# Moving three shared tiles of the first FFN behind its routed ones, with the attention's front steps re-placed around them

## The chip, the cores and the metric

One core of a Trainium2 chip runs the kernel. The metric is the device time of one execution in microseconds; here the median of three is given. The engines are TensorE (PE; its weight loads are PEld), VectorE (DVE), ScalarE (ACT), GpSimd (POOL) and SyncE (SP). SPq, ACTq and POOLq are instructions of an engine's queue that only issue DMAs. "L933" is line 933 of the kernel before.

## The reference

The block is x + 0.5 FFN(LN(x)), then x + attention(LN(x)), then x + 0.5 FFN(LN(x)), in float32, on 2 x 1024 tokens of width 128. The FFN has one shared expert and 7 routed ones of hidden width 352, of which each token uses two.

```python
def expert(h, g, u, d): return (silu(h @ g.T) * (h @ u.T)) @ d.T
def ffn(x):
    w = top2_normalised(softmax(x @ wr.T + rb))          # [tokens, 7], two non-zero
    return expert(x, sg, su, sd) + sum(w[:, e] * expert(x, rg[e], ru[e], rd[e]) for e in range(7))
def attention(x):
    v = x @ w_v + v_b
    q = (x @ w_q + q_b) @ w_k.T + k_b                      # keys are x itself
    scores = einsum(q, x) / sqrt(8)                        # 16 heads of 8, causal
    return softmax(scores) @ v @ c_proj_w + c_proj_b
x = x + 0.5 * ffn(layernorm(x)); x = x + attention(layernorm(x)); x = x + 0.5 * ffn(layernorm(x))
```

## The kernel before

**Tiles.** The 2048 tokens are 16 tiles of 128 and 4 chunks of 512. Chunks 0 and 1 are the first batch entry ("first half"), chunks 2 and 3 the second. Every engine has its own queue, written out in order by hand; between the queues there are only semaphores. Nothing is re-ordered at run time, so an instruction that waits holds all behind it on its engine.

**The FFN.** `ffn_pe`, `ffn_act` and `ffn_dve` walk the same 54 jobs (`JOBS`): 16 shared tiles ("s") and 38 routed ones ("r", `NJ`). In step q TensorE does the up projections of job q (`up_pe`, L899 to L901), the transposes of job q-1 (`act_tr_pe`, L919) and the down projection of job q-2 (`down_pe`, L933). `BEFORE[f]` says how many shared tiles run ahead of the routed ones: 16 (all) in the first FFN, 11 in the second. Other work is put in by step number: `FRONT_*` ahead of the step's job work, `BETWEEN_*` inside it, `BEHIND_*` after it.

**The routing.** The router's top two give each token two slots in lists sorted by expert. For each half GpSimd scatters the normalised rows to `z_rows` in memory: 32 indirect DMAs, 16 a half (`sort_pool`, L1174). Behind each but the first two of the 32 it runs a small memset as a pause (`pause_pool`, L1184). SP loads the sorted rows of each routed tile back (`rows_load_sp`, L1260). Tiles 0 to 9 need only the first half's sorts; tile 10 (`WHOLE`) and all after it need both. The tiles come in batches; `batch_at` gives the step in which a batch's rows are transposed (`rows_tr_pe`, L953). GpSimd scatters each routed result to `y_rows` (`scatter_pool`, L1197), the results come back (`results_load`, L1271) and are added with their weights: `mix_dve` for chunks 0 and 1, `weigh_both_act` and `add_both_pool` (L1138) for chunks 2 and 3.

**To the attention.** Each chunk's x is normalised (`n_stats` on VectorE, `n_z` on ScalarE), transposed (`n_tr`, L573), split in a high and a low part (`n_hi`, `n_lo`), and gives q (`q_pe`) and v (`v_pe`, L1508 to L1510, 12 matmuls a chunk). Queries and keys are stored to `q_stack` and `k_stack` and loaded in another layout. Chunks 0 and 1 do this inside the last FFN steps; chunks 2 and 3 need all routed results and do it inside the attention's prologue.

**The prologue** (`attn_pe`, `attn_dve`) is a ring of 54 entries `r` over four PSUM banks. TensorE makes scores (L1603), VectorE takes their maxima (L1756). Entries 0 to 37 are the first group's maxima; then come one of the next group, the two rows of maxima ("mrow", entries 39 and 40), and 13 more of the next group. `rows_load` brings the rows of maxima into the queries by DMA. `SECOND_PE` and `SECOND_DVE` say ahead of which entry a step of chunks 2 and 3 runs. From entry 45 TensorE also makes the main scores (`unit_pe`, L1646), and ScalarE takes the exponentials (L1815); from the fourth on, a score waits for the exponential three before it. Behind it the loop over 8 groups of heads runs.

```python
        if r == 2:
            e.wait_ge(K.A["qf"], 1)
        for step, c in SECOND_PE.get(r, ()):
            late_pe(K, 0, step, c)
        if r == UNITS_FROM:
            e.wait_ge(K.A["vev"], NCH)
            e.wait_ge(K.A["qf"], NCH)
```

ScalarE's queue at that place reads: end of the FFN, `v_act` of chunks 0 and 1, `results_load` of the second half, the scaling of its results, `n_z` and `n_hi` of chunks 2 and 3, `q_act(2)`, `keys_store(2)`, `q_act(3)`, `keys_store(3)`, `v_act` of 2 and 3, attention. SP's reads: keys and queries of chunks 0 and 1, their loads, `rows_load`, queries of chunks 2 and 3, and the clearing of the third key buffer.

Of the kernel before, what the change touches and what calls it, by code (L numbers as in the profile page):

```python
# [29 lines left out]
P = 128  # L30
# [52 lines left out]
BEFORE = (TT, 11)  # L83
# [16 lines left out]
ONE_AT_AGAIN = (46, NQ)  # L100
# [12 lines left out]
def batch_at(f, step):  # L113

    for b, (j, _) in enumerate(BATCHES):
        if step == BEFORE[f] + j - min(2 if f else b, 1 if j == WHOLE else 2):
            return b
    return None
# [136 lines left out]
MID_N_BANK, Q_BANK, V_BANK = (7, 6, 0, 1), (7, 6, 6, 4), (6, 4, 1, 0)  # L255
# [915 lines left out]
def sort_pool(K, f, g):  # L1171
# [4 lines left out]
    if g % TT > 0:  # L1176
        pause_pool(K, f == 1 and t < HALF)
# [335 lines left out]
def v_pe(K, c):  # L1513
    e = K.nc.tensor
    if c == 0:
        e.wait_ge(K.A["qf"], 2)
    elif c == 1:
        e.wait_ge(K.FF[0]["yev"], NQ)
    else:
        e.wait_ge(K.NS[1]["lo"], NCH)  # L1520
# [7 lines left out]
def q_pe(K, c):  # L1528
    e, cols = K.nc.tensor, slice(c * CHUNK, (c + 1) * CHUNK)
    e.wait_ge(K.NS[1]["lo"], c + 1)  # L1530
    if c >= 2:
        e.wait_ge(K.A["vev"], c - 1)
# [40 lines left out]
def stack_store(e, dram, part, c, src, s):  # L1573
    b, half = c // 2, c % 2
    dst = dram[b * HEADS:(b + 1) * HEADS, 8 + 8 * part:16 + 8 * part, half * CHUNK:(half + 1) * CHUNK]
    e.dma_start(dst, src.bitcast(F32)).then_inc(s, 16)  # L1576


def keys_store(K, e, c):
    cols = slice(c * CHUNK, (c + 1) * CHUNK)  # L1580
    e.wait_ge(K.NS[1]["lo"], c + 1)
    stack_store(e, K.k_dram, 0, c, K.zt_h[1][:, cols], K.k_st[c])
    stack_store(e, K.k_dram, 1, c, K.zt_l[1][:, cols], K.k_st[c])
    stack_store(e, K.k_dram, 2, c, K.zt_h[1][:, cols], K.k_st[c])


def queries_sp(K, c):
    e, u = K.nc.sync, c % 2
    e.wait_ge(K.A["ql"], c + 1)
    stack_store(e, K.q_dram, 0, c, K.q_h[:, u, :], K.q_st[c])  # L1590
    stack_store(e, K.q_dram, 1, c, K.q_h[:, u, :], K.q_st[c])
    stack_store(e, K.q_dram, 2, c, K.q_l[:, u, :], K.q_st[c])
# [122 lines left out]
SECOND_PE = {4: (("v", 0),), 6: (("v", 1),), 29: (("n_tr", 2),), 34: (("n_tr", 3), ("q", 2)), 40: (("q", 3),), 41: (("v", 2),),  # L1715
             43: (("v", 3),)}
SECOND_DVE = {22: (("n_stats", 2),), 25: (("n_stats", 3),), 31: (("n_lo", 2),), 37: (("n_lo", 3),)}
# [3 lines left out]
def attn_pe(K):  # L1721
    e = K.nc.tensor
    for r, (what, d, n) in enumerate(RING_PROLOGUE):
# [4 lines left out]
        elif r == 2:  # L1728
            e.wait_ge(K.A["qf"], 1)
# [629 lines left out]
```

## Time and profile before

| | |
|---|---|
| time, median of 3 (lowest to highest) | 573.25 us (572.37 to 575.6) |
| the profiled execution's own time | 573.25 us |
| its span | 571.4 us |
| TensorE busy | 524.7 us, 92% |
| VectorE, ScalarE, GpSimd busy | 68%, 56%, 48% |
| chain that ended last | PE 58%, issue 22%, DVE 6%, DMA 6%, SPq 5% |

The page cuts the span in 40 slices of 14.3 us; each digit is the busy share in tenths.

```profile
PE   6988889999697789999999999999999889899995
DVE  5696635467249759788888888879465776445744
PEclk9799989999958979999999999999999999999999
DMA  8922324134830582505050505020000131340414
```

The first FFN fills slices 0 to 10, the attention 10 to 29, the second FFN 29 to 39. TensorE's row falls to 6 in slice 10 and to 7 in slices 12 and 13; the clock row falls to 5 in slice 11. The costliest groups of the page, with their count, busy time, mean of one, and the idle time ahead of them:

```profile
L1756 DVE TENSOR_REDUCE mxp<-psum 128x1 f32<-128x512 f32 (+3 forms) x304 | 179.8, 655 | 47.4 <-PE psum L1603 34.6
L1646 PE MATMUL psum<-queries,keys 128*128 128x512 f32 (+3 forms) x384 | 124.0, 385 | 4.0 <-ACT probs L1815 3.8
L1603 PE MATMUL psum<-keys,queries 128*128 128x512 f32 (+1 forms) x304 | 119.4, 428 | 7.6 <-DMA queries<-q_stack 5.3
L933 PE MATMUL psum<-wall_f,at 128*128 (+1 forms) x648 | 91.0, 277 | 2.5 <-DVE x L1081 1.3
```

### The profile page before, as it was taken

Reading aid. Unit: us, or ns where it says so; the run is one execution under the profiler, and the core shown is the slowest. Engines: PE = TensorE matmul, PEld = TensorE weight load, DVE = VectorE, ACT = ScalarE, POOL = GpSimd, SP = SyncE. Lnnn points to the kernel's source line nnn. Section 1 sums busy time; section 2 is a strip of 40 time slices with the busy share of each in tenths; the row PEclk is TensorE's granted clock in tenths of the full one; section 3 lists DMA queues with packets and bytes.
Section 4 is the critical chain, followed back from the end, with each engine's and each line's share of the span. In section 5 each row is a group of like instructions: output and inputs, shape, how many; then the busy total and the mean of one; then the engine's idle time right before and its main releaser. Section 6 shows DMA issues by size and latency. Waiting matters only on the chain.

```text
span 571.4 us, 11375 instructions
## 1 busy us (share of the span) xinstructions
PE 524.7 (92%) x3574; PEld 408.8 (72%) x3574; DVE 386.8 (68%) x1013; ACT 320.0 (56%) x678; POOL 272.6 (48%) x417
## 2 busy tenths in 40 slices
PE   6988889999697789999999999999999889899995
PEld 2788879988563566666665656565745889899995
DVE  5696635467249759788888888879465776445744
ACT  4553434457205377676676767677777334344643
POOL 8299888766425510204040404020237888864540
PEclk9799989999958979999999999999999999999999
DMA  8922324134830582505050505020000131340414
GB/s 284 290 73 60 101 80 121 44 103 119 255 102 24 179 192 75 175 1 175 1 175 1 175 1 168 9 101 2 2 2 24 34 86 48 101 117 31 127 49 120
DMA packets 41384, 54.65 MB, mean 96 GB/s; under 512 B 6064, under 2 KB 32176, under 8 KB 40560
## 3 DMA queue, kind: packets, MB, share of 16 engines
q1 hardware_dynamic: 31664, 41.13, 25.2%
q0 software_dynamic: 4480, 9.25, 4.9%
q10 hardware_dynamic: 5184, 3.55, 2.2%
q8 instruction: 32, 0.52, 0.4%
q14 instruction: 24, 0.20, 0.1%
HBM read 34.03 MB, written 28.00 MB: 109 GB/s over the span
## 4 chain that ended last, share of the span: by engine, by line
PE 58%; issue 22%; DVE 6%; DMA 6%; SPq 5%; ACT 1%; ACTq 1%; POOL 1%; DVEq 0%; POOLq 0%
PE psum L1603 12%; PE psum L1646 11%; PE psum L1675 10%; PE psum L933 6%; PE psum L919 3%; PE psum L899 3%; PE psum L900 3%; PE psum L901 3%; PE psum L1606 3%; DVE mxp L1756 3%; DMA b_p<-in_attn_c_proj_b 2%; SPq L1260 1%; SPq L1576 1%; DMA queries<-q_stack 1%; SPq L1253 1%
## 5 line engine op out<-in xcount | busy, mean ns | idle before, releaser
L1756 DVE TENSOR_REDUCE mxp<-psum 128x1 f32<-128x512 f32 (+3 forms) x304 | 179.8, 655 | 47.4 <-PE psum L1603 34.6
L1815 ACT ACTIVATE probs<-psum 128x512 f32<-128x512 f32 (+1 forms) x304 | 155.3, 578 | 32.9 <-PE psum L1646 30.1
L1646 PE MATMUL psum<-queries,keys 128*128 128x512 f32 (+3 forms) x384 | 124.0, 385 | 4.0 <-ACT probs L1815 3.8
L1603 PE MATMUL psum<-keys,queries 128*128 128x512 f32 (+1 forms) x304 | 119.4, 428 | 7.6 <-DMA queries<-q_stack 5.3
L1862 POOL TENSOR_SCALAR_AFFINE_SELECT probs<-probs 128x512 f32<-128x512 f32 x64 | 40.0, 634 | 174.9 <-ACT probs L1815 174.9
L1000 ACT ACTIVATE silu<-psum 128x352 f32<-128x352 f32 x107 | 49.5, 463 | 95.9 <-PE psum L901 70.7
L1043 DVE TENSOR_TENSOR act<-silu,psum 128x352 f32<-128x352 f32 x107 | 55.6, 519 | 64.9 <-ACT silu L1000 41.3
L1197 POOL DMA_INDIRECT y_rows<-ys,to_row x76 | 74.3, 977 | 52.2 <-DVE ys L1079 26.6
L933 PE MATMUL psum<-wall_f,at 128*128 (+1 forms) x648 | 91.0, 277 | 2.5 <-DVE x L1081 1.3
L1646 PEld LDWEIGHTS psum<-queries,keys 128*128 128x128 f32 x384 | 68.0, 194 | 30.2 <-ACT probs L1815 16.3
L933 PEld LDWEIGHTS psum<-wall_f,at 128*128 128x128 f32 x648 | 80.9, 192 | 4.0 <-issue 1.8
L1603 PEld LDWEIGHTS psum<-keys,queries 128*128 128x128 f32 x304 | 60.1, 200 | 23.8 <-DVE mxp L1756 8.2
L1675 PE MATMUL psum<-probs,vg 128*32 128x512 f32 (+3 forms) x768 | 69.8, 491 | 0.4 <-POOL probs L1862 0.4
L919 PE MATMUL psum<-ident,act 128*128 128x128 f32 x324 | 54.2, 276 | 6.7 <-DVE act L1043 5.8
L1008 ACT COPY at<-psum 128x384 f32<-128x384 f32 x108 | 51.3, 475 | 11.4 <-PE psum L919 10.2
L899 PE MATMUL psum<-wall,zs_h 128*128 x152 | 55.9, 368 | 1.7 <-DVE zs_l L1067 1.7
L900 PE MATMUL psum<-wall,zs_h 128*128 x152 | 49.7, 327 | 0.0
L919 PEld LDWEIGHTS psum<-ident,act 128*128 128x128 f32 x324 | 40.7, 141 | 12.5 <-DVE act L1043 8.6
L901 PE MATMUL psum<-wall,zs_l 128*128 x152 | 49.5, 326 | 0.0
L1675 PEld LDWEIGHTS psum<-probs,vg 128*32 128x32 f32 x768 | 21.1, 109 | 35.4 <-issue 22.3
L1174 POOL DMA_INDIRECT z_rows<-zrow,slots x32 | 34.6, 1081 | 15.1 <-DVE slots L750 9.7
L1174 POOL DMA_INDIRECT z_rows<-zrow_late,slots x32 | 31.2, 975 | 5.8 <-issue 5.8
(240 smaller groups left out, 737.9 us busy)
## 6 DMA issues: line engine op xcount, KB each, us to landing
z_rows<-q_stack SPq DMA_DIRECT2D x12, 682.5 KB, 5.5
keys<-k_stack SPq DMA_DIRECT2D x32, 128.0 KB, 6.3
queries<-q_stack SPq DMA_DIRECT2D x8, 512.0 KB, 6.0
zg_early<-z_rows SPq DMA_DIRECT2D x44, 65.0 KB
yc<-y_rows SPq DMA_DIRECT2D x10, 256.0 KB, 4.4
zg_late<-z_rows SPq DMA_DIRECT2D x32, 65.0 KB
q_stack<-q_h SPq DMA_DIRECT2D x8, 256.0 KB, 4.7
keys<-q_stack SPq DMA_DIRECT2D x4, 512.0 KB, 8.1
```

The source lines that it names most:

```text
L899: e.matmul(dst, zh, weight(K.wall, base, hi, HID), start=True, stop=False)
L900: e.matmul(dst, zh, weight(K.wall, base, lo, HID), start=False, stop=False)
L901: ins = e.matmul(dst, zl, weight(K.wall, base, hi, HID), start=False, stop=True)
L919: ins = e.transpose(bank(K, at_bank(f, q))[:, k * P:(k + 1) * P], K.act[:, q % 2, k * P:(k + 1) * P], K.ident[:, :])
L933: ins = e.matmul(bank(K, Y_BANK)[:, 0:EMB], K.at[:, q % 2, k * P:(k + 1) * P], weight(K.wall_f, base, DN + k * EMB, EMB), start=(k == 0), ...
L1174: e.indirect_dma_start(K.z_dram[f], bass.IndirectOffsetOnAxis(ap=K.slots[:, g:g + 1], axis=0), K.zrow[f][:, t, :], None).then_inc(K.z_sc[t ...
L1197: e.indirect_dma_start(K.y_dram[f], bass.IndirectOffsetOnAxis(ap=K.to_row[:, j:j + 1], axis=0), K.ys[:, j % RING_Y, :], None).then_inc(K.y ...
L1603: ins = e.matmul(dst, K.queries[u][:, i * P:(i + 1) * P], K.keys[u][:, heads[0]:heads[-1] + 1, k0 * P:(k0 + nb) * P], start=True, stop=Tru ...
L1646: ins = e.matmul(slot(K, u, d, n)[:, m * (q1 - q0):(m + 1) * (q1 - q0)], K.keys[v][:, j, kt * P:(kt + 1) * P], K.queries[v][:, q0:q1], sta ...
L1675: ins = e.matmul(bank(K, O_BANK)[32 * j:32 * j + 32, q0 - half * CHUNK:q1 - half * CHUNK], K.vg[:, kt, j, :], probs_of(K, n)[:, j, :], sta ...
L1756: e.tensor_reduce(K.mxp[:, heads[0]:heads[-1] + 1, i, which], scores, AX.X, ALU.max).then_inc(K.A["taken"], 1)
L1815: e.activation(probs_of(K, product)[:, heads[0]:heads[-1] + 1, :], src, ACT.Exp, scale=SCALE).then_inc(K.A["ex"], 1)
```

## The change

Thirteen shared tiles of the first FFN run ahead of the routed ones and three behind them, instead of all 16 ahead. Steps tied to routed results (mix, statistics, `n_tr`, q of chunks 0 and 1) stand three steps earlier. The v products of chunks 0 and 1 move from ring entries 4 and 6 into steps 50 and 51. The steps of chunks 2 and 3 move to earlier ring entries (19 to 32 instead of 29 to 43 on TensorE, 13 to 26 instead of 22 to 37 on VectorE). The batch of tile 10 is transposed two steps ahead of its first job rather than one. The first FFN's sorts lose their pauses. The key stores of chunks 2 and 3 are issued by SP, ahead of the query stores, and `rows_load` comes behind them all. The four additions of the projection's bias run on GpSimd ahead of the attention loop instead of inside it. PSUM banks and waits are altered to match.

```diff
-BEFORE = (TT, 11)
+BEFORE = (13, 11)
...
-ONE_AT_AGAIN = (46, NQ)
+ONE_AT_AGAIN = (43, NQ)
...
-        if step == BEFORE[f] + j - min(2 if f else b, 1 if j == WHOLE else 2):
+        if step == BEFORE[f] + j - (min(b, 2) if f == 0 else 1 if j == WHOLE else 2):
...
-MID_N_BANK, Q_BANK, V_BANK = (7, 6, 0, 1), (7, 6, 6, 4), (6, 4, 1, 0)
+MID_N_BANK, Q_BANK, V_BANK = (7, 6, 0, 1), (7, 6, 6, 4), (7, 6, 1, 0)
...
-    if g % TT > 0:
+    if f == 1 and g % TT > 0:
...
 def v_pe(K, c):
     e = K.nc.tensor
     if c == 0:
+        e.wait_ge(K.A["qf"], 1)
+    elif c == 1:
         e.wait_ge(K.A["qf"], 2)
-    elif c == 1:
-        e.wait_ge(K.FF[0]["yev"], NQ)
...
-    if c >= 2:
-        e.wait_ge(K.A["vev"], c - 1)
+    if c == 2:
+        e.wait_ge(K.A["vev"], 2)
+    elif c == 3:
+        e.wait_ge(K.FF[0]["yev"], NQ)
...
-def keys_store(K, e, c):
-    cols = slice(c * CHUNK, (c + 1) * CHUNK)
+def keys_sp(K, c):
+    e, cols = K.nc.sync, slice(c * CHUNK, (c + 1) * CHUNK)
...
-SECOND_PE = {4: (("v", 0),), 6: (("v", 1),), 29: (("n_tr", 2),), 34: (("n_tr", 3), ("q", 2)), 40: (("q", 3),), 41: (("v", 2),),
-             43: (("v", 3),)}
-SECOND_DVE = {22: (("n_stats", 2),), 25: (("n_stats", 3),), 31: (("n_lo", 2),), 37: (("n_lo", 3),)}
+SECOND_PE = {19: (("n_tr", 2),), 24: (("n_tr", 3), ("q", 2)), 29: (("q", 3),), 30: (("v", 2),), 32: (("v", 3),)}
+SECOND_DVE = {13: (("n_stats", 2),), 16: (("n_stats", 3),), 20: (("n_lo", 2),), 26: (("n_lo", 3),)}
...
-            e.wait_ge(K.A["qf"], 1)
+            e.wait_ge(K.A["vev"], 1)
...
-    e.wait_ge(K.NS[1]["z"], NCH)
-            if 0 <= 3 * p + u - 1 < NCH:
-                proj_bias_pool(K, 3 * p + u - 1)
...
-        keys_store(K, e, c)
+        keys_sp(K, c)
...
     queries_load(K, 0, 0, 1)
-    rows_load(K, 0, 0, 0, RING_PROLOGUE.index(("mrow", 0, 0)))
+    for c in range(NCH // 2, NCH):
+        keys_sp(K, c)
     for c in range(NCH // 2, NCH):
         queries_sp(K, c)
+    rows_load(K, 0, 0, 0, RING_PROLOGUE.index(("mrow", 0, 0)))
     for c in range(NCH // 2, NCH):
         e.wait_ge(K.k_st[c], 16 * 3)
         e.wait_ge(K.q_st[c], 16 * 3)
...
-def proj_bias_pool(K, c):
-    xc = K.x[:, c * TPC:(c + 1) * TPC, :]
-    K.nc.gpsimd.tensor_tensor(xc, xc, K.b_p[:, :].unsqueeze(1).to_broadcast([P, TPC, EMB]), ALU.add)\
-     .then_inc(K.A["bp"], 1)
+def proj_bias_pool(K):
+    e = K.nc.gpsimd
+    e.wait_ge(K.NS[1]["z"], NCH)
+    for c in range(NCH):
+        xc = K.x[:, c * TPC:(c + 1) * TPC, :]
+        e.tensor_tensor(xc, xc, K.b_p[:, :].unsqueeze(1).to_broadcast([P, TPC, EMB]), ALU.add).then_inc(K.A["bp"], 1)
...
-FRONT_PE = {10: (("places", 1),), 47: (("n_tr", 0),), 48: (("q", 0),), 50: (("n_tr", 1),), 51: (("q", 1),)}
-BETWEEN_ACT = [{0: (("query", 0), ("hi0", 2)), 1: (("hi0", 3),), 48: (("q", 0),), 51: (("q", 1),)}, {}]
+FRONT_PE = {10: (("places", 1),), 44: (("n_tr", 0),), 45: (("q", 0),), 47: (("n_tr", 1),), 48: (("q", 1),),
+            50: (("v", 0),), 51: (("v", 1),)}
+BETWEEN_ACT = [{0: (("query", 0), ("hi0", 2)), 1: (("hi0", 3),), 45: (("q", 0),), 48: (("q", 1),)}, {}]
-               20: (("tanh", 0),), 42: (("weigh", 0),), 44: (("weigh", 1),), 45: (("n_z", 0),), 46: (("n_hi", 0),),
-               47: (("n_z", 1),), 49: (("n_hi", 1),)},
+               20: (("tanh", 0),), 39: (("weigh", 0),), 41: (("weigh", 1),), 42: (("n_z", 0),), 43: (("n_hi", 0),), 44: (("n_z", 1),),
+              46: (("n_hi", 1),), 50: (("v", 0),), 51: (("v", 1),)},
-BEHIND_DVE = [{0: (("query", 0),), **{2 * k + 3: (("weights_lo", m),) for k, m in enumerate(ROUTED_WEIGHTS)}, 19: (("small", 0),), 22: (("weights", 0),), 42: (("mix", 0),), 43: (("n_stats", 0),), 44: (("mix", 1),), 45: (("n_stats", 1),),
-               46: (("n_lo", 0),), 48: (("q_lo", 0),), 49: (("n_lo", 1),), 51: (("q_lo", 1),)},
+BEHIND_DVE = [{0: (("query", 0),), **{2 * k + 3: (("weights_lo", m),) for k, m in enumerate(ROUTED_WEIGHTS)}, 19: (("small", 0),), 22: (("weights", 0),), 39: (("mix", 0),), 40: (("n_stats", 0),), 41: (("mix", 1),), 42: (("n_stats", 1),), 43: (("n_lo", 0),),
+              45: (("q_lo", 0),), 46: (("n_lo", 1),), 48: (("q_lo", 1),)},
...
-            v_act(K, 0)
-            v_act(K, 1)
...
-            keys_store(K, e, 2)
-            keys_store(K, e, 3)
...
+            proj_bias_pool(K)
```

## Rows read from the trace of the kernel before

**Rows 1.** TensorE's timeline: start us, length us, engine, line, operation, count, [idle before it, releaser].
```profile
52.10 0.41 PE L899 MATMUL psum<-wall,zt_h 128*128 128x352 f32 x1
...
58.09 0.38 PE L953 MATMUL psum<-ident,zg_early 128*128 128x128 f32 x2
...
81.64 0.66 PE L953 MATMUL psum<-ident,zg_early 128*128 128x128 f32 x2 [2.65 <-DMA zg_early<-z_rows]
```

**Rows 2.** GpSimd's timeline, the sorting scatters.
```profile
26.94 0.96 POOL L1174 DMA_INDIRECT z_rows<-zrow,slots  x1 [0.30 <-issue]
...
44.28 2.37 POOL L1174 DMA_INDIRECT z_rows<-zrow,slots  x1 [0.17 <-issue]
...
50.37 0.96 POOL L1174 DMA_INDIRECT z_rows<-zrow,slots  x1 [0.16 <-issue]
...
75.71 0.96 POOL L1174 DMA_INDIRECT z_rows<-zrow,slots  x1 [0.17 <-issue]
```

**Rows 3.** TensorE's timeline, end of the first block.
```profile
151.80 0.93 PE L933 MATMUL psum<-wall_f,at 128*128 x6 [0.57 <-issue]
...
158.03 0.77 PE L1603 MATMUL psum<-keys,queries 128*128 128x512 f32 x1 [5.30 <-DMA queries<-q_stack]
```

**Rows 4.** Windows by stage: stretch, length, busy us per engine, granted clock, DMA share, GB/s.
```profile
158.00:172.70 14.70, 14.47 (x47) 10.24 (x47) 8.35 (x15) 2.15 (x6) 3.37 (x8) 0.60 0.36 105
```

**Rows 5.** VectorE's timeline between the blocks.
```profile
159.29 0.69 DVE L1756 TENSOR_REDUCE mxp<-psum 128x4 f32<-128x512 f32 x1 [6.04 <-PE psum L1606]
...
168.32 9.13 DVE L1756 TENSOR_REDUCE mxp<-psum 128x4 f32<-128x512 f32 x16 [2.58 <-PE psum L1606]
...
177.36 0.86 DVE L504 BATCH_NORM_STATS2 stats<-x 128x6 f32<-128x128 f32 x4
...
178.56 1.85 DVE L1756 TENSOR_REDUCE mxp<-psum 128x4 f32<-128x512 f32 x3
...
190.05 0.55 DVE L1756 TENSOR_REDUCE mxp<-psum 128x1 f32<-128x384 f32 x1
...
192.67 0.28 DVE L1770 CAST m_rows<-psum 32x128 fp32r<-32x128 f32 x1 [0.56 <-PE psum L1626]
```

**Rows 6.** ScalarE's timeline, the second half's results.
```profile
167.63 2.07 ACTq L1271 DMA_DIRECT2D yc<-y_rows  x4
...
171.72 4.79 ACT L1126 ACTIVATE yc<-yc,w 128x128 f32<-128x128 f32 x16 [3.80 <-DMA yc<-y_rows]
```

**Rows 7.** GpSimd's timeline, last scatters and the second half's additions.
```profile
148.85 0.96 POOL L1197 DMA_INDIRECT y_rows<-ys,to_row  x1 [1.97 <-DVE ys L1079]
...
153.34 0.96 POOL L1197 DMA_INDIRECT y_rows<-ys,to_row  x1 [0.55 <-issue]
...
173.14 5.34 POOL L1138 TENSOR_TENSOR x<-x,yc 128x512 f32<-128x512 f32 x4 [3.45 <-ACT yc L1126]
```

**Rows 8.** ScalarE's timeline, its first work of the attention.
```profile
200.23 1.28 ACT L1815 ACT_TABLE_LOAD   x1 [3.51 <-DMA k_stack<-zt_h]
```

**Rows 9.** TensorE's timeline, second half and main scores.
```profile
182.46 1.09 PE L573 MATMUL psum<-ident,z 128*128 128x128 f32 x4 [1.20 <-issue]
...
196.77 0.50 PE L1646 MATMUL psum<-queries,keys 128*128 128x512 f32 x1
...
202.17 0.80 PE L1646 MATMUL psum<-queries,keys 128*128 128x512 f32 x1 [3.58 <-ACT probs L1815]
```

**Rows 10.** SP's queue, loads of the second routed list.
```profile
78.39 9.02 SPq L1260 DMA_DIRECT2D zg_early<-z_rows  x12
```

**Rows 11.** VectorE's timeline, slot numbers of the second half.
```profile
47.64 0.55 DVE L750 CAST slots<-d_slot 128x16 int32<-128x16 f32 x1
```

**Rows 12.** TensorE's timeline, first and last of one chunk's 12 v matmuls.
```profile
192.39 0.31 PE L1508 MATMUL psum<-wv_h,zt_h 128*128 128x128 f32 x1
...
193.66 0.27 PE L1510 MATMUL psum<-wv_h,zt_l 128*128 128x128 f32 x1
```

**Rows 13.** SP's queue, the queries of chunks 0 and 1.
```profile
151.86 0.34 SPq L1930 DMA_DIRECT2D queries<-q_stack  x1
```

More of the change, by code:

```diff
@@ L1570, in q_dve, with stack_store @@
      .then_inc(K.A["ql"], 1)
-def stack_store(e, dram, part, c, src, s):
+def stack_store(K, dram, part, c, src, s):
     b, half = c // 2, c % 2
     dst = dram[b * HEADS:(b + 1) * HEADS, 8 + 8 * part:16 + 8 * part, half * CHUNK:(half + 1) * CHUNK]
-    e.dma_start(dst, src.bitcast(F32)).then_inc(s, 16)
-def keys_store(K, e, c):
-    cols = slice(c * CHUNK, (c + 1) * CHUNK)
+    K.nc.sync.dma_start(dst, src.bitcast(F32)).then_inc(s, 16)
+def keys_sp(K, c):
+    e, cols = K.nc.sync, slice(c * CHUNK, (c + 1) * CHUNK)
     e.wait_ge(K.NS[1]["lo"], c + 1)
-    stack_store(e, K.k_dram, 0, c, K.zt_h[1][:, cols], K.k_st[c])
-    stack_store(e, K.k_dram, 1, c, K.zt_l[1][:, cols], K.k_st[c])
-    stack_store(e, K.k_dram, 2, c, K.zt_h[1][:, cols], K.k_st[c])
+    stack_store(K, K.k_dram, 0, c, K.zt_h[1][:, cols], K.k_st[c])
+    stack_store(K, K.k_dram, 1, c, K.zt_l[1][:, cols], K.k_st[c])
+    stack_store(K, K.k_dram, 2, c, K.zt_h[1][:, cols], K.k_st[c])
 def queries_sp(K, c):
@@ L1589, in queries_sp @@
     e.wait_ge(K.A["ql"], c + 1)
-    stack_store(e, K.q_dram, 0, c, K.q_h[:, u, :], K.q_st[c])
-    stack_store(e, K.q_dram, 1, c, K.q_h[:, u, :], K.q_st[c])
-    stack_store(e, K.q_dram, 2, c, K.q_l[:, u, :], K.q_st[c])
+    stack_store(K, K.q_dram, 0, c, K.q_h[:, u, :], K.q_st[c])
+    stack_store(K, K.q_dram, 1, c, K.q_h[:, u, :], K.q_st[c])
+    stack_store(K, K.q_dram, 2, c, K.q_l[:, u, :], K.q_st[c])
 def m_unit_pe(K, n, r_bank, u):
```

## The prediction, as put on record before the run

> **What bounds the kernel now.** I read the 40 slices of the page first, then the windows by stage, then TensorE's timeline around the two places where it idles, and last the timelines of the engine that released it. The kernel is three blocks in a row (first FFN, attention, second FFN), and TensorE's queue runs through all of them in a written order. In the attention loop (about 210 to 410 us) and in both FFN loops TensorE is busy in nearly all of every slice, so a moved job there is worth nothing by itself. What is left to win lies at two seams.
>
> The first seam is the rows of the second routed list. A routed tile can start only when its sorted rows are back from memory. TensorE stands 2.65 us at 81.64 for them [rows 1], because GpSimd issues the 32 sorting scatters at one per 1.57 us up to 75.71 [rows 2].
>
> The second seam is FFN to attention, 152.7 to 202.2 us. TensorE ends its last down projection at 151.80 + 0.93 = 152.7 and begins the first score at 158.03, after 5.30 us of waiting for the queries [rows 3]; the clock granted in the next stretch is 0.60, most of it at the 1.2 GHz level [rows 4]. VectorE then takes maxima one by one, stands while TensorE makes v (2.58 us at 168.32 for one chunk) [rows 5], and the second half of the tokens is late: its results are fetched at 167.63 [rows 6], though the last scatter was issued at 153.34 [rows 7]. So ScalarE is let go only at 200.23 and TensorE goes on at 202.17 [rows 8, 9]. From there the loop is full. The forecast is therefore: by how much does the matmul at 202.17 move?
>
> **The change part by part, first block.** Routed jobs begin at step 13 instead of 16, and the pauses behind 30 of the 32 sorting scatters go. Jobs, weights and matmuls stay the same in number; three shared jobs (about 2.0 us each: 58.09 - 52.10 over three steps [rows 1]) pass from ahead of the routed ones to behind them. So all rows are wanted earlier: tile 0 at step 13, i.e. at 52.1, and tile 10 at step 21 instead of 25.
>
> Pace of the sorts. A scatter without a pause follows the last by 0.96 + 0.30 = 1.26 us (the third sort, 26.94); with one, 0.96 + 0.17 + 0.43 (the pause) = 1.57. That is 0.31 a piece. The first half has 13 pauses ahead of its 16th sort, now at 50.37: it moves to 46.3 [rows 2]. SP's first load starts 1.7 us behind the end of the last sort (76.7 to 78.39 [rows 10]) and TensorE goes on 3.25 us after that (81.64), so the first rows are there at 47.3 + 1.7 + 3.25 = 52.2: no stall at 52.1, or 0.1. The second half cannot start before its slot numbers, written at 47.64 + 0.55 = 48.2 [rows 11]; with 0.8 us of hand-over it starts at 49.0 instead of 51.9 (50.37 + 1.57), and its 15 steps take 18.9 + 0.3 (it now holds one slow one) = 19.2: the last sort is at 68.2, not 75.71, so 7.5 us earlier. Tile 10's rows then serve TensorE at 81.64 - 7.5 = 74.1.
>
> TensorE's side. It needs 20.9 us from 58.09 to the beginning of the stall at 78.99, nine jobs and three batch fronts; one job fewer makes 18.9, and it arrives at 52.1 + 18.9 = 71.0. It stalls 3.1 us instead of 2.65, and has 33 jobs ahead of it instead of 29: 74.1 + 4 x 2.0 = 82.1 against 81.64. First block, before anything else: +0.5 us (slower). Both ends: if the unpaused pace meets nothing new and the hand-over is 0.3, 0.0; if each half has two more slow sorts like the one at 44.28 (2.37 us instead of 0.96 [rows 2]), +3. The list work of VectorE in steps 14 to 18 now shares these steps with batch work; it is hidden by the stall at step 21.
>
> One rule of the Trainium skill speaks against dropping the pauses. In the trace the sort at 44.28 takes 2.37 us where its neighbours take 0.96 [rows 2]. "SBUF — State Buffer", section "SBUF: two separate sides", says that VectorE and GpSimd share a port pair as an exclusive lock, and that GpSimd cannot write descriptors for its DMAs while VectorE holds it. By that rule the slow ones belong to long VectorE casts of weights, whose number the change leaves alone, and the sum stays; were the pauses what lets VectorE in, its small operations would be late instead.
>
> **The seam.** The v products of chunks 0 and 1 go from the attention prologue to steps 50 and 51. In the trace 12 matmuls of v take 193.66 - 192.39 over 11 spacings = 0.115 us each at full clock [rows 12]; 24 make 2.8 us, and they are on the path there. The block's end is 152.7 + 0.5 + 2.8 = 156.0.
>
> The queries of chunks 0 and 1 are made three steps earlier. SP's load at 151.86 [rows 13], which lets TensorE go at 158.03, moves by 3 x 2.0 less 0.5: rows there at 152.5, hidden behind the block's end. The 5.3 us stall goes; next late is the block's end itself, so scores start at 156.0, 2.0 us earlier, and VectorE's first maximum at 159.29 - 2.0 = 157.3 [rows 5].
>
> The second half. Job 50 now is the last routed one; its scatter is today at 148.85 [rows 7], with the shifts at 152.2. Done at 153.1, landed 1.7 later as the sorts did: 154.8. ScalarE no longer stands behind v (its queue held the fetch until 167.63) and fetches at once; 4.1 us later the scaling starts (167.63 to 171.72 [rows 6]), 158.9, and GpSimd's additions 1.4 later, 160.3, the first chunk ready 2.7 later (four take 5.34 [rows 7]), 163.0, the second at 165.7. VectorE comes to the statistics behind 13 maxima instead of 22: 16 maxima take 9.13 us, 0.571 each [rows 5], so 157.3 + 7.4 = 164.7, and to the second ones at 164.7 + 1.2 + 3 x 0.571 = 167.6. Both chunks are ready in time by 1.7 us. The transposes follow the start of the statistics by 182.46 - 177.36 = 5.1 us [rows 5, 9], at 169.8; VectorE has its three buffered maxima until 170.5.
>
> VectorE's work to the two rows of maxima: 38 maxima x 0.571 = 21.7, two statistics of 1.2 (177.36 to the next maximum at 178.56), two low parts of 0.6 (counted as a maximum of that size), and from the last maximum's end (190.60) to the second row's end (192.95) 2.35 us [rows 5]: 27.7 in all. New holes: transposes, q and two v (2.8 us) now fall into the middle of the maxima, with three to four maxima (2 us) buffered: I take 3.5 us, between 1.5 and 6 (6 if the v run at the lower clock, twice 1.4 us more). Second row: 157.3 + 27.7 + 3.5 = 188.5. Today 192.95.
>
> From there to the matmul of 202.17. The first score of the main pass needs this row back through a DMA: at most 196.77 - 192.95 = 3.8 us, as its own queue held it until then [rows 9]; at least 1 us. I take 2.0. Then one score (0.50), one exponential of its size and the way between the engines to the fourth score, which waits for it: 1.5 us taken; up to 1.3 more if the table load of 1.28 us [rows 8] cannot be done ahead. 188.5 + 2.0 + 1.5 = 192.0, against 202.17: 10.2 us.
>
> What is cost at nothing. The key stores of chunks 2 and 3 pass from ScalarE's queue to SP's, ahead of the query stores and of the row load: SP idles there today, the last store is out near 183, five us before the rows. Query stores of chunk 3 wait there for GpSimd. If they were late they would hold the row load behind them on SP, which nothing in the sum does. The bias additions on GpSimd (four of 1.3 us, by its other additions of that size) come after v, near 184 to 189, and the first mask is due after 192; behind them wait the value copy and the masks only. The altered bank for v and the earlier single bank for the act transposes cost nothing while ScalarE keeps its place.
>
> Sum: 573.25 us of the profiled execution - 10.2 = **563.0 us**. That execution is also the median of the runs shown; its span is 571.4.
>
> **Rivals.**
> A. The seam is only half won: v and q fall at the 1.2 GHz level and the row's DMA takes its upper bound. Holes 6 and not 3.5, row 3.8, table load 1.3 in the way: 2.5 + 1.8 + 1.3 = 5.6 less, 568.6; two of the three make 566.5. For it speaks the low clock of the stretch [rows 4], against it that the 5.3 us idle stretch ahead of it goes.
> B. Without pauses the sorts go no faster (the change does not do what it does on paper). Tile 10's rows come at 81.64 still, TensorE stands 10.6 us, the first block is 8.0 later rather than 0.5: 563.0 + 7.5 = 570.5. For it: only one back-to-back sort is among the rows; against it, the gap of 0.30 us ahead of it is all that it needed.
> C. The other side: back-to-back descriptor work and VectorE hold each other up. If each of the 16 sorts of the second half takes as the one at 44.28, 2.37 + 0.17 = 2.5 us, the half takes 38 us, the last sort is at 49.0 + 38.1 = 87.1, tile 10 starts at 93.0 and the block ends 19 us later: 581.5, slower. It decides from a pace of about 1.9 us on (68.2 + 10.2 = 78.4 for the last sort). Against it: only one sort of that length among those of [rows 2], and with the pauses in the 16 spacings from 50.37 to 75.71 average 1.58.
> D. More than forecast: the fourth score at 202.17 takes 0.80 where the one at 196.77 takes 0.50 [rows 9], because TensorE had idled. If the start of the loop runs at full clock, some 2 us more are won: 561.
>
> **How the numbers follow.** Forecast with D's share 0.63 (560 to 566), A 0.19 (566 to 569), B 0.09 (569 to 572), C and like collisions 0.07, something better than 560 0.02. Range 560 to 568, which takes in the likelier half of A and leaves out about 0.2. What can be told from no change is 0.5%, 2.9 us: faster means below 570.4. That is 0.63 + 0.19 + 0.02 and near half of B, 0.87; same 0.06 (rest of B, mild C), slower 0.07.
>
> **What would show it.** Sorts 1.26 us apart and the last near 68; one TensorE stall for loaded rows near 71 to 74; the first score near 156 with no stall for queries; results fetched near 155; the transposes of chunk 2 near 170; the fourth main score near 192 and everything behind it shifted by one amount. The forecast is wrong if the last sort is later than 72, if VectorE waits for statistics input, or if the loop's length itself changes.

## The result, with the profile after

The changed kernel takes 579.34 us (median of 18 runs, 576.25 to 582.2) against 575.45 us of the kernel before in the same sessions (18 runs, 570.88 to 578.81): ratio 1.0075, 95% interval 1.0053 to 1.0096. It is slower by 0.75%, where 563.0 was forecast. Its profiled execution took 579.51 us with a span of 577.7.

The page's slices of the changed kernel, as before in 40 (14.4 us each):

```profile
PE   5976479999996799999999999999999889889995
POOL 8374727777445730303030303030327888844540
PEclk9998679999996989999999999999999999999999
```

The reader is to see a new hole in slices 3 to 5, from 43 to 87 us (6, 4 and 7 tenths where TensorE was at 8 before), and that the old hole of slice 10 is gone. Those of slices 12 and 13 are still there (6 and 7 tenths, 7 and 7 before). The loops behind have their old length: the fourth main score is 6.0 us late and the span 6.3.

GpSimd's timeline of the changed kernel, sorting scatters (the second one, which has no pause ahead of it in either kernel, then the last of the first half, and the first and last of the second half), answers to [rows 2]:

```profile
24.91 0.96 POOL L1174 DMA_INDIRECT z_rows<-zrow,slots  x1 [0.30 <-issue]
...
44.94 0.96 POOL L1174 DMA_INDIRECT z_rows<-zrow,slots  x1 [0.30 <-issue]
...
52.65 0.95 POOL L1174 DMA_INDIRECT z_rows<-zrow,slots  x1 [6.75 <-DVE slots L750]
...
71.58 0.96 POOL L1174 DMA_INDIRECT z_rows<-zrow,slots  x1 [0.30 <-issue]
```

The pace is the forecast one, 1.26 us, and the last sort is 4.1 us earlier than before, where 7.5 was forecast. But the slots of the second half came 4.0 us late (51.66 against 47.64 in [rows 11]). In the same stretch the timelines of VectorE, ScalarE and TensorE:

```profile
61.24 0.29 DVE L1081 SCALAR_TENSOR_TENSOR x<-psum,x 128x128 f32<-128x128 f32 x1 [4.73 <-remote]
63.07 0.42 DVE L1067 TENSOR_TENSOR zs_l<-psum,zs_h 128x256 fp32r<-128x256 f32 x1 [1.54 <-issue]
68.84 0.52 DVE L1043 TENSOR_TENSOR act<-silu,psum 128x352 f32<-128x352 f32 x1 [5.35 <-issue]
75.39 0.29 DVE L1081 SCALAR_TENSOR_TENSOR x<-psum,x 128x128 f32<-128x128 f32 x1 [6.04 <-remote]
```

```profile
62.66 0.37 ACT L1017 CAST zs_h<-psum 128x256 fp32r<-128x256 f32 x1 [5.24 <-remote]
68.34 0.46 ACT L1000 ACTIVATE silu<-psum 128x352 f32<-128x352 f32 x1 [5.31 <-remote]
74.64 0.48 ACT L1008 COPY at<-psum 128x384 f32<-128x384 f32 x1 [5.84 <-remote]
```

```profile
55.88 0.38 PE L953 MATMUL psum<-ident,zg_early 128*128 128x128 f32 x2
63.63 0.66 PE L899 MATMUL psum<-wall,zs_h 128*128 x1 [7.38 <-DVE zs_l L1067]
...
65.55 0.84 PE L919 MATMUL psum<-ident,act 128*128 128x128 f32 x3
66.19 1.49 PE L933 MATMUL psum<-wall_f,at 128*128 128x128 f32 x6
...
75.22 0.87 PE L919 MATMUL psum<-ident,act 128*128 128x128 f32 x3 [5.15 <-issue]
```

Here "remote" means that the profile finds no instruction whose end explains the release. The transposes at 55.88 end at 56.3, and ScalarE, which waits for nothing else, reads them at 62.66. The instructions themselves are as short as ever (0.29, 0.52); what takes 5 to 6 us is the wait ahead of them. From 75.4 on, 2.9 us behind the end of the last sort, all goes at the old pace. I call this the hold-up.

All three engines stand, but only one signal is late. Follow the job. ScalarE's cast at 62.66 comes 6.4 us behind the TensorE transposes that it reads. VectorE's L1067 then starts 0.04 us behind the end of that cast, and TensorE's L899 0.14 us behind the end of L1067. In the same way ScalarE's copy at 74.64 reads the transposes of 65.55 (ended 66.39), TensorE starts at 75.22, 0.10 us behind the end of that copy, and VectorE's L1081 at 75.39 reads the matmuls of 66.19 (ended 67.68). So TensorE's own waits, 7.38 and 5.15 us, are waits for the others, who were waiting for TensorE. With the jobs matched in this way from 8 to 92 us, what ScalarE and VectorE signal is taken up within 0.24 us in every one of the 20 traces (the two kernels and the eighteen runs below), in the hold-up too; what TensorE signals is taken up as much as 5.3 to 12.2 us late in the eleven with the hold-up, and in the other nine never more than 1.33 us late (late from the moment when the producer had ended and the reader was free). Within a run of scatters the lateness grows: 1.2 us at 33.9, 2.9 at 41.3, 3.3 at 47.1, and after the gap between the halves again from 1.0 at 57.0 to 6.0 at 75.4. The profile works out the ends of matmuls, so it doesn't tell whether the signal or the matmul's own end was late. Windows by stage (busy time of TensorE, its weight loads, VectorE, ScalarE, GpSimd; granted clock; DMA share; GB/s), first the kernel before:

```profile
52.00:76.00 24.00, 22.34 (x172) 21.89 (x171) 15.54 (x52) 10.22 (x25) 21.52 (x31) 1.00 0.35 91
```

and the changed kernel:

```profile
52.00:76.00 24.00, 10.62 (x55) 9.94 (x56) 3.97 (x14) 3.28 (x8) 15.32 (x16) 0.73 0.28 78
```

TensorE does 55 matmuls in place of 172. The DMA engines are, in the mean of the 16, no busier than before, so their time is not the thing that is full. The clock follows: TensorE has idled, and the granted clock averages 0.73.

The seam, TensorE of the changed kernel, answers to [rows 3, 9]:

```profile
168.81 0.91 PE L933 MATMUL psum<-wall_f,at 128*128 128x128 f32 x6 [0.48 <-DVE x L1081]
169.47 0.47 PE L1605 MATMUL psum<-keys,queries 128*128 128x512 f32 x1
...
184.85 1.08 PE L573 MATMUL psum<-ident,z 128*128 128x128 f32 x4 [3.39 <-issue]
...
203.10 0.58 PE L1628 MATMUL psum<-ident,mm_hl 128*32 128x128 f32 x2 [3.48 <-DVE mm_hl L1765]
...
208.16 0.39 PE L1648 MATMUL psum<-queries,keys 128*128 128x512 f32 x1
```

and VectorE, answers to [rows 5]:

```profile
170.33 7.33 DVE L1757 TENSOR_REDUCE mxp<-psum 128x4 f32<-128x512 f32 x13
178.44 0.87 DVE L504 BATCH_NORM_STATS2 stats<-x 128x6 f32<-128x128 f32 x4 [0.78 <-POOL x L1138]
...
200.54 1.18 DVE L1763 CAST mm_hl<-nmax 128x32 fp32r<-128x32 f32 x1
201.76 1.19 DVE L1765 TENSOR_TENSOR mm_hl<-nmax,mm_hl 128x32 fp32r<-128x32 f32 x1
```

GpSimd and ScalarE in the same seam, answers to [rows 6, 7]:

```profile
165.58 0.96 POOL L1197 DMA_INDIRECT y_rows<-ys,to_row  x1 [1.02 <-DVE ys L1079]
...
175.72 5.32 POOL L1138 TENSOR_TENSOR x<-x,yc 128x512 f32<-128x512 f32 x4 [5.83 <-ACT yc L1126]
...
199.21 4.92 POOL L2060 TENSOR_TENSOR x<-x,b_p 128x512 f32<-128x512 f32 x4
```

```profile
170.22 2.07 ACTq L1271 DMA_DIRECT2D yc<-y_rows  x4
```

No stall for the queries is left. VectorE's two small operations, a cast and a subtraction, lie inside GpSimd's bias additions (four of 1.23 us, 199.21 to 204.1), and each ends as one of these ends. From the block's end to the fourth main score it is 208.16 - 169.72 = 38.4 us, against 202.17 - 152.73 = 49.4 before: 11.0 us won. The first block gives back 17.0 (169.72 - 152.73), of which 2.8 are the v products moved there. 17.0 - 11.0 = 6.0, the shift.

### The profile page after: what moved, and what is told of

It is laid out like the page before. It is cut to its first block, busy times and chain, and to the rows that moved or that the text cites. A ratio compares the mean times of both kernels' runs of the same rounds, so it can differ in the third digit from the quotient of the medians.

```text
span 577.7 us, 11344 instructions
## 1 busy us (share of the span) xinstructions
PE 521.8 (90%) x3574; PEld 406.3 (70%) x3574; DVE 388.1 (67%) x1013; ACT 320.2 (55%) x678; POOL 258.4 (45%) x387
## 3 DMA queue, kind: packets, MB, share of 16 engines
q10 hardware_dynamic: 4320, 1.98, 1.4%
## 4 chain that ended last, share of the span: by engine, by line
PE 62%; issue 18%; DVE 6%; DMA 5%; another core or an unknown queue 3%; ACT 3%; SPq 2%; POOL 0%; ACTq 0%; DVEq 0%; POOLq 0%
PE psum L1648 11%; PE psum L1605 11%; PE psum L1677 10%; PE psum L933 8%; PE psum L901 4%; PE psum L919 4%; PE psum L899 4%; PE psum L900 4%; PE psum L1608 2%; DMA yc<-y_rows 2%; DMA y_rows<-ys,to_row 1%; DMA nat_route<-in_ffn_wr 1%; DVE mxp L1757 1%; PE psum L1633 1%
## 5 line engine op out<-in xcount | busy, mean ns | idle before, releaser
L1648 PE MATMUL psum<-queries,keys 128*128 128x512 f32 (+3 forms) x384 | 122.4, 380 | 0.6 <-DMA queries<-m_rows 0.2
L1605 PE MATMUL psum<-keys,queries 128*128 128x512 f32 (+1 forms) x304 | 116.1, 418 | 2.6 <-DVE mxp L1757 2.2
L933 PE MATMUL psum<-wall_f,at 128*128 (+1 forms) x648 | 93.3, 281 | 5.6 <-issue 3.2
L933 PEld LDWEIGHTS psum<-wall_f,at 128*128 128x128 f32 x648 | 82.4, 195 | 8.3 <-issue 5.3
L1648 PEld LDWEIGHTS psum<-queries,keys 128*128 128x128 f32 x384 | 66.7, 190 | 26.7 <-ACT probs L1816 12.6
L1605 PEld LDWEIGHTS psum<-keys,queries 128*128 128x128 f32 x304 | 58.4, 195 | 17.8 <-DVE mxp L1757 7.5
L899 PE MATMUL psum<-wall,zs_h 128*128 x152 | 56.7, 373 | 7.5 <-DVE zs_l L1067 7.5
L919 PEld LDWEIGHTS psum<-ident,act 128*128 128x128 f32 x324 | 41.3, 143 | 20.0 <-DVE act L1043 10.0
L900 PE MATMUL psum<-wall,zs_h 128*128 x152 | 50.3, 331 | 0.0
L1174 POOL DMA_INDIRECT z_rows<-zrow,slots x32 | 33.3, 1040 | 24.4 <-DVE slots L750 15.3
L899 PEld LDWEIGHTS psum<-wall,zs_h 128*128 128x128 f32 x152 | 29.6, 195 | 8.2 <-issue 8.1
```

The costliest lines, as they stand in the source:

```text
L899: e.matmul(dst, zh, weight(K.wall, base, hi, HID), start=True, stop=False)
L900: e.matmul(dst, zh, weight(K.wall, base, lo, HID), start=False, stop=False)
L919: ins = e.transpose(bank(K, at_bank(f, q))[:, k * P:(k + 1) * P], K.act[:, q % 2, k * P:(k + 1) * P], K.ident[:, :])
L933: ins = e.matmul(bank(K, Y_BANK)[:, 0:EMB], K.at[:, q % 2, k * P:(k + 1) * P], weight(K.wall_f, base, DN + k * EMB, EMB), start=(k == 0), ...
L1605: ins = e.matmul(dst, K.queries[u][:, i * P:(i + 1) * P], K.keys[u][:, heads[0]:heads[-1] + 1, k0 * P:(k0 + nb) * P], start=True, stop=Tru ...
L1648: ins = e.matmul(slot(K, u, d, n)[:, m * (q1 - q0):(m + 1) * (q1 - q0)], K.keys[v][:, j, kt * P:(kt + 1) * P], K.queries[v][:, q0:q1], sta ...
```

## The experiments

Eighteen runs in five sessions, each on a chip of its own, called A to E in the order below; ratios are against the kernel before on the same chip. Each chip was used in one session only, so "the chip" below is the chip or the moment.

**Chip A: put pauses back, take them from the kernel before.**

```diff
-    if f == 1 and g % TT > 0:
+    if g % TT > 0:                               # e1, on the changed kernel
+    if g % TT > 0 and (f == 1 or t < HALF):      # e3, on the changed kernel
+    if g % TT > 0 and (f == 1 or t >= HALF):     # e4, on the changed kernel
```

```diff
-    if g % TT > 0:
+    if f == 1 and g % TT > 0:                    # e2, on the kernel before
```

> The changed kernel with the pause behind each sorting scatter put back, everything else as changed. Theory T (scatters issued back to back by GpSimd hold up the waits of the other engines): sorts 1.57 us apart, last near 76, no wait of 5 us for a release between 52 and 73; tile 0's rows reach TensorE near 56 and tile 10's near 82, so the first block ends near 163.5 (8 us of waiting for rows and 2.8 of v products), the fourth main score is 38.4 us later as in the changed kernel, near 202, and the time is that of the kernel before, 571 to 575. Rival R (the pauses have no part in it; the routed jobs three steps earlier, and the key stores and bias additions that were moved, cost the time): first block ends near 170 as in the changed kernel, time 577 to 581.

Measured: 571.53 us, ratio 0.9998 (0.9959 to 1.0037). Sorts 1.56 us apart; stalls for rows of 4.92 us at 54.87 and 4.43 at 80.25; block's end 161.3, fourth main score 199.8. As T says.

> The kernel before with only the pauses of the first FFN's sorting scatters taken out. T: the slots of the second half come near 51.7 instead of 47.6, the second half's sorts run from 52.6 to 72, TensorE, VectorE and ScalarE stand in waits of about 5 us in that stretch and lose five to six jobs of 2.0 us: the first block ends 10 to 14 us later, time 583 to 589. R: sorts end 7 us earlier, the stall of 2.65 us at 81.64 goes, time 570 to 573.

Measured: 567.88 us, ratio 0.9863 (0.9814 to 0.9911): faster. T fails here. The sorts go at 1.26 us and TensorE is busy 22.34 of the 24 us from 52 to 76, as with pauses.

> The changed kernel with pauses behind the sorts of the first half of the tokens only; the second half goes back to back. T: slots at 47.6 again, second half's sorts 51.9 to 71, the 5 us waits in that stretch stay, first tile's rows near 56; about as slow as the changed kernel, 577 to 582. R: as the changed kernel, 579.

Measured: 564.61 us, ratio 0.9844 (0.9772 to 0.9915), block's end 156.0, fourth main score 196.55. Neither theory: no wait for "remote" in the unpaused second half.

> The changed kernel with pauses behind the sorts of the second half only. T: the small delays of 0.7 to 1.2 us between 36 and 45 stay and the slots come near 51.7, but no wait of 5 us is left; last sort near 77, first block ends near 165, time 572 to 576. R: 579 as the changed kernel.

Measured: 566.99 us, ratio 0.9889 (0.9810 to 0.9968), slots at 45.77 and not 51.7; no "remote" wait either, though up to the 17th sort this kernel issues the same work in the same order as the changed one.

**Chip B: is it the program or the chip?**

```diff
-    if f == 1 and g % TT > 0:
+    if g % TT > 0 and (f == 1 or g % 4 == 3):    # e6: both scatters of every fourth tile
```

e5 is the changed kernel itself. e7 moves `proj_bias_pool` back into the attention loop. e8 has `BEFORE = (TT, 11)`, the transposes and queries three steps later, v of chunk 0 at step 50, v of chunk 1 at ring entry 4.

> The changed kernel, unaltered, once more. The four kernels so far, each with some or all sorts back to back, showed no wait of 5 us for a release. Theory H (the hold-up belongs to this program: both halves back to back and the routed jobs at step 13): waits of about 5 us between 57 and 75 again, block end near 170, 576 to 582. Theory K (it belonged to the chip or the moment of that measurement): sorts 1.26 us apart, tile 0's rows near 52, block end near 154, fourth main score near 194, 562 to 567.

Measured: 584.69 us, ratio 1.0178 (1.0102 to 1.0254); the hold-up is there, slots at 52.84, stalls of 5.99 and 7.15 us on TensorE, block's end 171.1.

> The changed kernel with a pause behind every fourth sort only (8 in place of 30). Both theories: last sort near 71. H, if the hold-up builds up in an unbroken run of sorts: gone, 562 to 567. H, if it hangs on the order alone: 576 to 582. K: 562 to 567 like the changed kernel itself.

Measured: 582.7 us, 1.0148 (1.0068 to 1.0229); a stall of 8.87 us at 65.23, block's end 169.5. Eight pauses that come in pairs don't help.

> The changed kernel with the bias additions of GpSimd back in the attention loop. In the seam the two casts of the maxima beside them take 0.2 us instead of 1.2: the fourth main score 2 us sooner behind the block's end than in the changed kernel. For the hold-up in the first block: H says it stays (576 to 580), unless it hangs on where the instructions lie; K says it is not there (560 to 565).

Measured: 578.59 us, 1.0059 (1.0027 to 1.0091); hold-up there, block's end 172.6, the cast takes 0.18 us, and the fourth main score comes 37.0 us behind the block's end, 39.0 in e5 beside it. The 2 us are shown.

> The changed kernel with the routed jobs from step 16 again, sorts back to back, v of chunk 0 at step 50 and v of chunk 1 in the attention prologue: the seam's other moves stay. H and K: no stall for rows; first block ends near 152, a stall of 4 to 5 us for the queries comes back, first score near 156, fourth main score near 195, 564 to 568. If the hold-up came from back-to-back sorts beside the list work alone: 575 or more.

Measured: 593.39 us, 1.0329 (1.0261 to 1.0396); stalls of 4.01, 8.26 and 5.29 us, block's end 172.0. Yet until step 49 it does the work of e2, which had no hold-up on chip A. That points to the chip.

**Chip C: the same kernels as on chip A.** e9 is the changed kernel, e10 is e2, e11 is e3; e12 is e1 with the bias additions back in the loop.

> The changed kernel, unaltered, beside the next three on one chip. The four kernels that ran on the first chip showed no hold-up, the four on the second (all with sorts back to back) all but certainly one, and two of them, the unpaused kernel before and the changed kernel with routed jobs from 16, have the same work up to 140 us. Theory K (whether the hold-up comes is a property of the chip or moment, given sorts back to back): this kernel and the next two all show it or none does. Theory H (a property of the program): this one shows it, 576 or more, and the next one does not, 566 to 572.

Measured: 582.94 us, 1.0108 (1.0071 to 1.0144), with the hold-up, block's end 173.7.

> The kernel before without the pauses of the first FFN, once more. K: if the changed kernel beside it shows the hold-up, this one too, waits of 5 us, 585 to 595 (as the changed kernel with routed jobs from 16: 593); if not, 566 to 570. H: 566 to 570 in either case.

Measured: 593.97 us, 1.0268 (1.0194 to 1.0342). One program, 1.4% faster than before on A and 2.7% slower on C. Its windows from 26 to 76, first on A:

```profile
26.00:52.00 26.00, 22.89 (x171) 21.79 (x169) 20.19 (x64) 13.91 (x26) 19.22 (x17) 0.98 0.31 79
52.00:76.00 24.00, 22.34 (x171) 21.81 (x170) 15.02 (x49) 10.09 (x25) 18.85 (x22) 1.00 0.40 107
```

then on C, and GpSimd's first sort of the second half there (on A it waited 1.98 us, at 50.81):

```profile
26.00:52.00 26.00, 16.00 (x96) 14.69 (x95) 9.63 (x31) 8.25 (x15) 16.00 (x16) 0.75 0.30 76
52.00:76.00 24.00, 16.62 (x113) 14.88 (x111) 12.53 (x38) 7.44 (x15) 9.06 (x10) 0.93 0.28 73
```

```profile
64.20 0.96 POOL L1174 DMA_INDIRECT z_rows<-zrow,slots  x1 [17.64 <-DVE slots L750]
```

The hold-up delays its own cause: the unpaused first half delays VectorE, which writes the slots that the second half waits for.

> The changed kernel with pauses in the first half of the sorts only, once more. K: if the hold-up is there, it stands in the second half, from 52 to 72, and costs 10 us and more: 575 to 585; if not, 563 to 566. H: 563 to 566.

Measured: 579.95 us, 1.0068 (1.0043 to 1.0093). Up to 52 nothing; then, in the windows on A and on C:

```profile
52.00:76.00 24.00, 18.62 (x121) 18.05 (x122) 12.42 (x42) 7.49 (x17) 18.63 (x22) 0.86 0.41 103
```

```profile
52.00:76.00 24.00, 10.71 (x51) 9.54 (x49) 3.31 (x14) 2.15 (x5) 18.03 (x20) 0.65 0.32 85
```

So K holds: given back-to-back sorts, the chip (or what its session brought) decides. The second half shows the hold-up by itself (e11); in e9 and e10 it begins in the first.

> The changed kernel with all pauses put back and the bias additions back in the attention loop. Both theories: no hold-up on any chip. First block ends near 161.3 and, with the additions away from the two casts, the fourth main score comes 36.5 to 37.5 us later instead of 38.4: near 198, 568 to 572. If the additions now delay the masks of the first steps instead: no gain over the kernel with pauses alone, 571.

Measured: 570.86 us, 0.9889 (0.9806 to 0.9972), no "remote" wait on a chip whose other three kernels had them; the latest signal of TensorE is taken up 1.33 us late, 0.05 in e1 on A. Against e9 two things differ, the pauses and the bias additions, and e7 shows that moving the additions leaves the hold-up: the pauses remove it. VectorE's two small operations beside no GpSimd addition:

```profile
192.66 0.18 DVE L1763 CAST mm_hl<-nmax 128x32 fp32r<-128x32 f32 x1
192.88 0.19 DVE L1765 TENSOR_TENSOR mm_hl<-nmax,mm_hl 128x32 fp32r<-128x32 f32 x1
```

Block's end 161.9, fourth main score 198.2: 36.4 us. This version beats both kernels on the same chip, by 1.1% the one before and by 2.1% the changed one (570.86 against 582.94).

**Chip D: how long a pause?**

```diff
-    if f == 1 and g % TT > 0:
-        pause_pool(K, f == 1 and t < HALF)
+    if g % TT > 0:
+        pause_pool(K, f == 1 and t < HALF, PAUSE if f else 8)     # e14; 128 in e15
```

e13 is the changed kernel as control; e16 has pauses of 384 columns, the additions in the loop and `BEFORE = (15, 11)` with the tied steps two later.

> The changed kernel, unaltered, as the control for the next two on the same chip. On a chip with the hold-up: waits of 5 us for a release during the second half of the sorts, first block's end near 170, 578 to 585. On a chip without it: first block's end near 154 to 157, 562 to 567.

Measured: 583.64 us, 1.0112 (1.0037 to 1.0188), hold-up there, block's end 172.3.

> The changed kernel with a pause of 8 columns (in place of 384) behind 30 sorts of the first FFN. Theory B (the break between two scatters is what lets the others in): sorts about 1.3 us apart, no wait of 5 us, tile 0's rows near 53, first block's end near 157, 564 to 568. Theory L (it takes the length, GpSimd must be away from scatters for a time): waits of 5 us as in the control, within 1% of it.

Measured: 584.04 us, 1.0147 (1.0079 to 1.0216), TensorE stalls 8.52 us at 77.21. The sorts start 1.27 us apart, so the short break hardly changes the pace, and it does nothing.

> The same with a pause of 128 columns. B: like 8 columns, sorts 1.35 to 1.4 us apart, 565 to 569. L with a threshold between 128 and 384 columns: as the control; below 128: 565 to 569, while 8 columns still shows the waits.

Measured: 580.9 us, 1.0087 (1.0052 to 1.0122). The sorts of the second half start 1.35 us apart, and the waits of 52 to 76 are still there:

```profile
53.28 0.96 POOL L1174 DMA_INDIRECT z_rows<-zrow,slots  x1 [1.76 <-DVE slots L750]
54.25 0.22 POOL L1184 MEMSET idle<- 128x128 bf16 x1
54.63 0.97 POOL L1174 DMA_INDIRECT z_rows<-zrow,slots  x1 [0.16 <-issue]
```

```profile
DVE x L1081 <- remote: 9.7, 1, 9.7
DVE act L1043 <- issue: 7.0, 2, 5.5
PEld psum L919 <- issue: 5.7, 1, 5.7
```

So it takes length: 0.39 us between scatters is too little, 0.60 (0.43 + 0.17) is enough in e12 on C and e16 on D (TensorE's latest signal 1.33 and 1.08 us late). Whether the gap counts or the pace, 1.35 against 1.56 us, these runs don't separate.

> The changed kernel with all pauses of 384 columns, the bias additions in the loop, and routed jobs from step 15 instead of 13. No hold-up on any chip. The two stalls for rows (4.7 and 4.8 us from step 13) fall to under 1 and about 4; first block's end near 158, a stall for queries of at most 1 us, fourth main score near 195, 566 to 570, 2 to 3 us faster than from step 13.

Measured: 572.65 us, 0.9929 (0.9891 to 0.9967). The first stall for rows goes, the second is 6.02 us at 81.54, the queries cost 1.26; block's end 158.2 but fourth main score only at 200.4. Expected 566 to 570: missed, the seam took 42 us, not 37. TensorE is busy 1.6 of the 10 us from 168.2 on there, 5.7 in the same stretch behind the block's end in e12; why isn't shown. No better than from 13.

**Chip E: bytes or scatters?** e17 is the changed kernel with rows of 66 columns (the scatter, its DRAM rows and their loads; cleared columns in place of the rest, so it leaves out half the features of the routed tokens and its result is not the block's); e18 is e4.

```diff
-                         K.zrow[f][:, t, :], None).then_inc(K.z_sc[t // HALF], 16)
+                         K.zrow[f][:, t, 0 if f else EMB // 2:ROW], None).then_inc(K.z_sc[t // HALF], 16)
```

> The changed kernel (no pauses in the first FFN) with sorted rows of 66 columns instead of 130: the first 64 of the 128 features of each routed token are left out (they count as zero), so each scatter moves half the bytes with as many rows. Theory D (the bytes of the scatters at this pace fill something that the other engines' signals share): waits of 5 us gone, first block's end near 157, 563 to 568. Theory S (it hangs on the scatters' instructions and descriptors, not on the bytes): sorts of 0.96 + 0.30 us, waits of 5 us as with whole rows, first block's end near 170, 577 to 585. On a chip without the hold-up, as the second kernel would show, nothing follows.

Measured: 560.34 us, 0.9747 (0.9695 to 0.9800), no hold-up. TensorE's timeline:

```profile
53.86 0.41 PE L955 MATMUL psum<-ident,zg_early 128*128 128x128 f32 x2 [1.31 <-DMA zg_early<-z_rows]
...
74.21 0.41 PE L955 MATMUL psum<-ident,zg_early 128*128 128x128 f32 x2 [1.84 <-DMA zg_early<-z_rows]
```

> The changed kernel with pauses behind the sorts of the second half only, as once before on a chip without the hold-up (567.0). On a chip with it: waits of 2 to 4 us for a release between 35 and 48, slots of the second half near 51.5 instead of 46, none after that; last sort near 77, first block's end 160 to 164, 571 to 576. The difference to the changed kernel, 6 to 10 us, is what the second half costs.

Measured: 566.2 us, 0.9862 (0.9806 to 0.9918), slots at 45.45, no "remote" wait: the control shows that E is a chip like A. So D and S are not told apart. What e17 does show is the forecast's first block without hold-up, all sorts unpaused (last at 68.88), though with half the bytes to land: block's end 154.7, fourth main score 194.6.

## Why the prediction was wrong

**The step that failed** is the first block's sum, "+0.5 us (slower). Both ends: ... 0.0 ... +3". Measured without the v products: 17.0 - 2.8 = +14.2. Within it:

- Pace of the sorts: right (1.26 us, on every chip). Rival B falls.
- The neighbours of the sorts: wrong. The upper end priced only slower sorts. The sentence "were the pauses what lets VectorE in, its small operations would be late instead" came nearest to what happened, but the sum gave it nothing and the chances at most a part of the 0.07 of "C and like collisions". What the runs showed in its place: on some chips, while the scatters go out every 1.26 us, TensorE's signals are taken up to 6.0 us late (12.2 in e11), VectorE and ScalarE stand for them, TensorE for those two, and the block ends 14.2 us later than the v products explain. Rival C has nearly the right time (581.5) by a wrong mechanism: not one of the second half's 16 sorts was slow, and it was to decide from a pace of 1.9 us. What was slow was the way from TensorE to its readers.
- The rule that I weighed, "SBUF — State Buffer", section "SBUF: two separate sides" of the Trainium skill, a port pair shared by VectorE and GpSimd alone, does not cover it: what is late are TensorE's signals, to ScalarE as to VectorE, while VectorE's operations there are as short as ever. It does fit the other small surprise: the cast and the subtraction beside GpSimd's bias additions took 1.18 and 1.19 us, 0.18 and 0.19 without. And the slow sorts are where the prediction put them: in both kernels those of 1.65 to 2.37 us begin within 0.8 us of VectorE's L1482 on the weights (1.25 or 1.61 us), which are subtractions and not casts; there are three in each.
- Stalls for rows: forecast 0 to 0.1 at 52.1 and 3.1 near 71 to 74. Without hold-up (e17, with half the bytes) 1.31 at 53.86 and 1.84 with the start at 74.21, forecast 74.1.

**The seam** was forecast as 156.0 to 192.0, 36.0 us; measured 38.4. The bias additions, costed at nothing "near 184 to 189", came at 199.2 to 204.1, since GpSimd's queue held them behind v, which itself came later than forecast, and cost 2.0 on VectorE: with them in the loop it is 36.4 to 37.0 (e12, e7). No stall for queries: right. First maximum 0.6 us behind the block's end for 1.3. The last scatter took 3.7 us to land (166.5 to the fetch at 170.2), not 1.7, so the slack of 1.7 us was gone and VectorE stood 0.78, the prediction's own sign "if VectorE waits for statistics input". Statistics to transposes 6.4 us for 5.1, since GpSimd is still adding until 181.0 before it can make the scale. The table load was done ahead, as hoped. These small ones nearly cancel: the second row of maxima came 34.4 us behind the block's end (forecast 32.5), its DMA took 2.4 (2.0), the way to the fourth score 1.6 (1.5). The forecast seam is 2.4 too short, 2.0 of it the additions. Where the hold-up was not in the way it is worse: in e3, e4, e17 and e18, which have the additions where the changed kernel has them, the seam took 40.0 to 41.6 us (38.5 in e1). VectorE stood 1.5 to 2.1 us for the results there, and the granted clock of the last 10 to 12 us was 0.66 to 0.71, against 0.80 in the changed kernel.

**The whole.** Forecast -10.2: first block +0.5, v +2.8, seam -13.4 (49.4 to 36.0). Measured at the fourth main score +6.0: +14.2, +2.8, -11.0. On chips A and E the kernels nearest to the changed one took 0.9747 to 0.9889 of before; the changed kernel itself was never run there, so that it would have been about 563 is likely and not shown. Had it come out so, the sum would have been right partly by luck: e17, the nearest, ends its first block 1.3 us sooner than forecast and needs 4.0 us more for the seam.

**Left open:** what makes TensorE's signals late, and whether it is the signal or the end of the matmul. It is not the DMA engines' time (0.28 against 0.35), and not an instruction of ScalarE or VectorE that got longer. Whether bytes or descriptors count, and what differs between A, E and the others, I can't say; a third pause length between 128 and 384 columns wasn't run either.

## What to carry to other kernels

Price a gap between DMAs that GpSimd issues by what the other engines do in it, not by the scatters alone: here 0.31 us a scatter was saved and 14 us lost. Where several engines at once wait for releases that the trace can't explain, match producer and reader job by job to find whose signal is late, look for a queue that issues without a break, and compare the same program on more than one chip before believing either sign. And a job that is hidden in a full loop (the bias additions) is not hidden at a seam, even on an engine that seems free there.

## What the runs showed of the hardware

- Indirect scatters of 128 rows of 520 bytes issued by GpSimd every 1.26 to 1.35 us made TensorE's signals to ScalarE and VectorE up to 5.3 to 12.2 us late on three of five chips (B, C, D), and not more than 0.05 on two (A, E); at 1.56 us apart not more than 1.33 anywhere. The signals of ScalarE and VectorE were never more than 0.24 us late.
- The same program (e2, e10) ran 1.4% faster than the kernel before on one chip and 2.7% slower on another, while the kernel before itself agreed within 0.6% there (572.88, 575.87).
- A VectorE cast of 128x32 beside GpSimd's additions took 1.18 us for 0.18, once (e4) 3.98.
- The six sorting scatters of the kernel before and the changed kernel that took 1.65 to 2.37 us for 0.96 all began beside VectorE's L1482, a subtraction of 128x1056 or 128x1408.
